# Twelve tile slots in place of six in the expert stage of a gated cross-attention and mixture-of-experts block

## The chip, the cores and the metric

One core of one Trainium2 chip. The metric is the time of the program on the device in microseconds (us), the median of several runs; lower is better.

## The reference

Input `x` has 64 batches of 128 tokens with 128 features. Two residual steps follow each other: cross-attention to a context, then a feed-forward block in which each token goes through one shared expert and one routed expert.

```python
x = x + jnp.tanh(g_xattn[0]) * _L0_xattn_ref(ctx_1024, _layernorm(x, axis=-1), ctx_1024, ...)
x = x + jnp.tanh(g_ffn[0]) * _L0_ffn_ref(_layernorm(x, axis=-1), ...)
...
h = (x - mu) / jnp.sqrt(var + LN_EPS) * ln_gamma + ln_beta
shared_out = jax.nn.silu(jnp.einsum('btd,fd->btf', h, sw1)) @ sw2.T
probs = jax.nn.softmax(h @ router_w.T, axis=-1)
top_prob = jnp.max(probs, axis=-1)
top_idx = jnp.argmax(probs, axis=-1)
h1 = jax.nn.silu(jnp.einsum('btd,efd->ebtf', h, ew1))
eo = jnp.einsum('ebtf,edf->ebtd', h1, ew2)
gate = jax.nn.one_hot(top_idx, N_EXPERTS, dtype=h.dtype) * top_prob[..., None]
routed_out = jnp.einsum('ebtd,bte->btd', eo, gate)
return shared_out + routed_out
```

There are 8 routed experts with 256 hidden features; all expert weights are rounded to three values (-1, 0, 1) times a scale per row.

## The kernel before, in words

The program has two stages. In the attention stage, about the first 420 us of the trace, every batch passes through attention, and each finished token row (128 features, three numbers that its later steps need, and its token number: `ROW` = 132 values) is stored to a buffer in HBM, `rows`, at a place sorted by its expert (`store_rows`, L431). Each expert has a region of its own there.

In the expert stage the sorted rows are worked through as tiles of 128 rows of one expert. There are `NT` = 72 tiles, taken two at a time: 36 pairs, numbered n = 0 to 35. For each pair the engines do this, in this order:

- SP (L291 to L301) reads the two tiles' places from the table `tile_row` and starts two loads from `rows` into slot k of `tin` (L297), 66 KB each. Slot k = n mod `SLOTS`.
- DVE normalises both tiles into `xh` (`normalise_tile`, L754), once the loads have landed.
- PE transposes them (`transpose_tile`, L1284); ACT copies the result to `hT` with the layer norm's gain and offset (`copy_tileT`, L970); DVE splits it in three bf16 parts (`split`, L764).
- PE multiplies with the first-layer weights, shared and routed (`first_layer`, L1292); ACT applies silu (`silus`, L977); PE multiplies with the second layer (`second_layer`, L1311).
- DVE adds both results to the tile in `tin` and writes slot k of `res` (`combine`, L778).
- POOL does a tiny addition into `carrier` (L464), which is held until `res` is there, and then issues two indirect writes of the rows of `res` to `out`, one for each tile, by the token numbers in `tin` (L474). Their landing counts up the semaphore `out_done[k]`.

Each engine has its own program and goes through it strictly in order. All of them write the pairs out in groups of `SLOTS`, with `NG` = 36 / `SLOTS` groups. PE, ACT and DVE have the first and the last group written out and those between as the body of a hardware loop (`Fori`); SP has the first group written out and the others as a loop, POOL has one loop for all groups. A slot number is thus fixed in the code. At the start of a group PE and ACT read the expert numbers of all its tiles from the table `tile_e` into registers with one instruction (L1280 and L997); PE reads the four of the group before again.

On DVE the order within step k is: normalise pair k + 2, split pair k + 1, combine pair k - 1. On PE it is: transpose pair k + 1, first layer of pair k, second layer of pair k - 1. Between the engines the intermediate tiles (`xh`, `hT`, `hpart`, the PSUM banks, `h1s` and `h1r`) have two buffers each, whatever `SLOTS` is; only `tin`, `res` and the semaphores `tile_in` and `out_done` are there once for each slot.

A slot can be loaded again when its results have been written out. This is the wait that SP has in every group but the first:

```python
            def group(g, first=False):
                for k in range(SLOTS):
                    if not first:
                        sp.wait_ge(out_done[k], 32 * g)
                    for a in range(2):
                        row = sp.value_load(tile_row[0:1, bass.ds((g * SLOTS + k) * 2 + a, 1)], ...)
                        sp.dma_start(tin[:, k, a, :], A["rows"][bass.ds(row, P), :]).then_inc(tile_in[k], 16)
```

and this is where DVE waits for the load, at the head of its step:

```python
                dve.wait_ge(tile_in[k], 32 * (g + 1))
                ge(dve, tileT_psum, n - 1)
```

Of the kernel before, what the change touches and what calls it, by code (L numbers as in the profile page):

```python
# [41 lines left out]
PARTS = 3  # L42
MR = P - SK
PAYS = 4
SLOTS = 6
NG = NT // 2 // SLOTS
LAST_SUMS, LAST_PROJ, LAST_RANKS, LAST_LOGITS = 4, 5, 0, 1
SP_PADS = 4
# [10 lines left out]
def build(nc, A):  # L59
    ctx = ExitStack()  # L60
    with ctx:
        def sb(name, shape, dt=FP32):
            return ctx.enter_context(nc.sbuf_tensor(name, shape, dt))

        def sem(name):
            return ctx.enter_context(nc.semaphore(name))
# [114 lines left out]
        h1r = shared[:, 4 * F:8 * F].rearrange("p (s a f c) -> p s a f c", s=2, a=2, f=FB)  # L181
        res = sb("res", [P, SLOTS, 2, D])
        W2T = sb("W2T", [P, NE, FB, P])
        neg = sb("neg", [P, F])
        W1T = sb("W1T", [P, NE, FB, P], BF16)
        tin = sb("tin", [P, SLOTS, 2, ROW])
        rest = sb("rest", [P, 2 * P])
# [36 lines left out]
        pads_out, carried = sem("pads_out"), sem("carried")  # L224
        tile_in = [sem(f"tile_in{k}") for k in range(SLOTS)]
        xh_ready, tileT_psum, tileT_copied, h_part, split_done = (sem(x) for x in ("xh_ready", "tileT_psum", "tileT_copied", "h_part", "split_done"))
        zs_psum, zr_psum, silu_done, y_psum, y_sum, res_ready = (sem(x) for x in ("zs_psum", "zr_psum", "silu_done", "y_psum", "y_sum", "res_ready"))
        out_done = [sem(f"out_done{k}") for k in range(SLOTS)]

# [5 lines left out]
        def _(sp):  # L235
# [55 lines left out]
# [5 lines that stand above are left out]
                        row = sp.value_load(tile_row[0:1, bass.ds((g * SLOTS + k) * 2 + a, 1)], min_val=0, max_val=E * REGION)  # L296
                        sp.dma_start(tin[:, k, a, :], A["rows"][bass.ds(row, P), :]).then_inc(tile_in[k], 16)  # L297
# [1078 lines left out]
```

## Time and profile before

| what | us |
|---|---|
| runs | 582.95, 587.7, 588.3 |
| median of the runs | 587.7 |
| span of the profiled execution | 583.8 |
| attention stage and tables in that span | 0 to about 425 |
| first load of a tile in the expert stage | 425.5 |
| first result handed to POOL | 440.7 |
| last result handed to POOL | 574.4 |

The profile follows one execution of the program. Engines are named PE (matmul), PEld (its weight loads, which overlap PE), DVE, ACT, POOL and SP; a "q" behind a name is the engine's own instruction queue. Times in the trace are counted from the start of the span. The profiled execution's own time is its span, 583.8 us, between the lowest and the median of the three runs and 3.9 us below the median.

### The profile page before, as it was taken

What the parts mean: (1) busy time and instruction counts of PE and PEld (TensorE: products, weight loads), DVE (VectorE), ACT (ScalarE), POOL (GpSimd) and SP (SyncE); (2) the same over time, 40 slices, a digit from 0 to 9 for tenths busy, and PEclk for the clock granted to TensorE, in tenths of its full rate; (3) what the DMA queues carried; (4) which work ended last, traced back from release to release, by engine and by line L of the source; (5) the groups of instructions that cost most, each with busy time, mean ns of one, the idle gap of its engine ahead of it and who ended that gap; (6) DMA issues with size and microseconds to landing.
All of it is one profiled execution on the core that took longest, in us unless ns stands there. A gap on an engine that the chain in (4) does not pass through costs nothing.

```text
span 583.8 us, 22049 instructions
## 1 busy us (share of the span) xinstructions
PE 533.3 (91%) x8243; PEld 438.6 (75%) x8244; DVE 434.6 (74%) x1245; ACT 309.2 (53%) x686; POOL 374.4 (64%) x842
## 2 busy tenths in 40 slices
PE   3869999999999999999999999998889899989991
PEld 1347777878778788888888888886558888888881
DVE  3269666788888889888777777777857777777771
ACT  1415555555555556666565565443136666666660
POOL 7653465476777777877867867767604656565564
PEclk9868999999999999999999999999789999999997
DMA  6900431110211202202202102000221222222210
GB/s 169 244 9 5 135 101 39 57 56 23 67 36 45 72 12 70 72 12 71 62 21 71 55 28 64 13 17 29 85 47 52 67 58 70 69 67 64 71 56 10
DMA packets 53578, 34.61 MB, mean 59 GB/s; under 512 B 6034, under 2 KB 50910, under 8 KB 53488
## 3 DMA queue, kind: packets, MB, share of 16 engines
q1 hardware_dynamic: 47104, 24.38, 15.7%
q0 software_dynamic: 4352, 8.53, 4.4%
q8 instruction: 61, 1.00, 0.7%
q10 hardware_dynamic: 2032, 0.46, 0.4%
q14 instruction: 29, 0.24, 0.1%
HBM read 24.22 MB, written 9.65 MB: 58 GB/s over the span
## 4 chain that ended last, share of the span: by engine, by line
PE 53%; issue 18%; POOL 12%; DVE 10%; DMA 2%; ACT 1%; POOLq 1%; SPq 1%; ACTq 0%; DVEq 0%
PE PS L1108 12%; POOL out L474 9%; PE PS L1078 8%; PE PS L1061 8%; PE PS L1091 7%; PE PS L1048 5%; PE PS L1135 4%; DVE nm L554 2%; DVE rinv L562 2%; POOL rows L434 2%; DVE st L501 2%; PE PS L1069 1%; PE PS L1042 1%; POOL carrier L464 1%; DMA mask_i<-in_mask 1%
## 5 line engine op out<-in xcount | busy, mean ns | idle before, releaser
L894 ACT ACTIVATE shared<-PS 104x768 f32<-104x768 f32 x128 | 103.6, 809 | 62.4 <-PE PS L1091 62.2
L554 DVE TENSOR_REDUCE nm<-PS 128x8 f32<-128x616 f32 x128 | 102.2, 799 | 37.8 <-PE PS L1061 32.0
L1078 PE MATMUL PS<-xT,kbd 32*104 32x128 f32 x1536 | 117.9, 285 | 0.0
L1061 PE MATMUL PS<-kbd,xT 32*128 32x308 f32 x512 | 103.8, 482 | 0.0
L474 POOL DMA_INDIRECT out<-res,tin x72 | 75.0, 1042 | 30.3 <-issue 30.3
L1078 PEld LDWEIGHTS PS<-xT,kbd 32*104 32x104 f32 x1536 | 90.8, 167 | 0.1
L562 DVE RECIPROCAL rinv<-PS 128x128 f32<-128x128 f32 x64 | 61.3, 957 | 25.8 <-PE PS L1108 24.9
L434 POOL DMA_INDIRECT rows<-X,pos_i x64 | 66.0, 1031 | 17.7 <-issue 7.5
L1091 PEld LDWEIGHTS PS<-moving,pairsel 128*104 128x104 bf16 x768 | 56.3, 128 | 15.3 <-issue 12.5
L1091 PE MATMUL PS<-moving,pairsel 128*104 128x128 bf16 x768 | 66.9, 223 | 0.0
L405 POOL CAST nm<-nm 128x16 bf16<-128x16 f32 x64 | 13.3, 208 | 77.4 <-DVE nm L554 77.3
L1048 PE MATMUL PS<-maskneg,identb 128*128 128x308 bf16 x256 | 56.2, 302 | 6.7 <-DVE nm L554 6.5
L1061 PEld LDWEIGHTS PS<-kbd,xT 32*128 32x128 f32 x512 | 39.3, 188 | 22.2 <-issue 17.5
L1108 PE MATMUL PS<-shared,own 104*32 104x128 f32 x1536 | 55.4, 277 | 0.3 <-ACT shared L894 0.3
L1108 PE MATMUL PS<-shared,vm 104*32 104x128 f32 x1536 | 53.6, 273 | 0.0
L985 ACT ACTIVATE shared<-PS,wabs 128x256 f32<-128x256 f32 x72 | 34.0, 474 | 27.2 <-PE PS L1299 19.4
L351 POOL TENSOR_TENSOR kbd<-kp,rowsel 128x308 f32<-128x308 f32 x64 | 44.8, 702 | 2.1 <-ACT kp L883 2.1
L1318 PE MATMUL PS<-W2T,shared 128*128 128x128 f32 x288 | 45.9, 282 | 0.0
L1108 PEld LDWEIGHTS PS<-shared,own 104*32 104x32 f32 x1536 | 38.2, 110 | 9.2 <-ACT shared L894 0.4
L1322 PE MATMUL PS<-W2T,shared 128*128 x288 | 43.9, 275 | 0.0
L1108 PEld LDWEIGHTS PS<-shared,vm 104*32 104x32 f32 x1536 | 43.2, 110 | 0.0
L760 DVE TENSOR_SCALAR xh<-tin 128x128 f32<-128x128 f32 x72 | 22.7, 368 | 26.0 <-DMA tin<-rows 25.9
(202 smaller groups left out, 1093.1 us busy)
## 6 DMA issues: line engine op xcount, KB each, us to landing
ctxq<-in_ctx SPq DMA_DIRECT2D x32, 154.0 KB
tin<-rows SPq DMA_DIRECT2D x72, 66.0 KB, 1.8
X<-in_x SPq DMA_DIRECT2D x8, 512.0 KB, 7.1
ctxp<-in_ctx SPq DMA_DIRECT2D x16, 154.0 KB
ctxq<-in_ctx SPq DMA_DIRECT2D x16, 104.0 KB
ctxq<-in_ctx SPq DMA_DIRECT2D x16, 102.0 KB
out<-res,tin POOLq DMA_INDIRECT x72, 2.3
w2n<-in_ew SPq DMA_DIRECT2D x1, 1024.0 KB, 6.0
```

What stands on the lines that cost most here:

```text
L351: nc.gpsimd.tensor_tensor(kbd[:, q % 2, j, :, 0:SK], kp[:, j].unsqueeze(1).broadcast_to([P, GH, SK]), rowsel[:].unsqueeze(2).broadcast_to( ...
L434: nc.gpsimd.indirect_dma_start(out=A["rows"][:, :], out_offset=row_of(pos_i[:, b:b + 1]), in_=X[:, b, :], in_offset=None).then_inc(sorted_ ...
L474: nc.gpsimd.indirect_dma_start(out=A["out"].rearrange("b q d -> (b q) d"), out_offset=row_of(tin[:, k, a, ROW - 1:ROW]), in_=res[:, k, a, ...
L554: nc.vector.tensor_reduce(nm[:, b % 2, 2 * u * GH:2 * (u + 1) * GH].rearrange("p (g i) -> p g i", g=2), PS[:, 0:2, 0:GK].rearrange("p g (i ...
L562: nc.vector.reciprocal(rinv[:], PS[:, bank, P:2 * P]).then_inc(rinv_done, 1)
L894: nc.scalar.activation(PT[:, b % 2, 2 * u:2 * u + 2, :], PS[0:CR, 2 + 2 * u:4 + 2 * u, 0:CH * P], ACT.Exp, scale=float(1.0 / np.sqrt(HD))) ...
L1048: nc.tensor.matmul(PS[:, v, 0:GK], identb[:], maskneg[:].rearrange("p i k -> p (i k)"), start=True, stop=False)
L1061: ins = nc.tensor.matmul(PS[:, v, 0:GK].rearrange("p (i k) -> p i k", k=SK), xT[r, q % 2, j * P:(j + 1) * P], kbd[r, q % 2, j, :, 0:SK], s ...
L1078: nc.tensor.matmul(PS[0:CR, 2 + g, c * P:(c + 1) * P], kbd[r, q % 2, j].rearrange("p i k -> p (i k)")[:, c * CR:(c + 1) * CR], xT[r, q % 2 ...
L1091: ins = nc.tensor.matmul(PS[0:CR, 2 + g, c * P:(c + 1) * P], pairsel[:, g].rearrange("p i k -> p (i k)")[:, c * CR:(c + 1) * CR], moving[: ...
L1108: ins = nc.tensor.matmul(PS[g * GR:(g + 1) * GR, bank, col:col + P], w[:, c, :] if col else w[:, c, g, :], PT[:, b % 2, g, c * P:(c + 1) * ...
L1318: nc.tensor.matmul(PS[:, 4 + s, 2 * a * P:(2 * a + 1) * P], h1s[:, s, f, a * P:(a + 1) * P], W2T[:, E, f, :], start=f == 0, stop=f == FB - 1)
```

## The change

One constant goes from 6 to 12. With it `tin` and `res` have twelve slots in place of six (and `tile_in` and `out_done` twelve semaphores each), and `NG` goes from six groups of six pairs to three groups of twelve.

```diff
-SLOTS = 6
+SLOTS = 12
 NG = NT // 2 // SLOTS
```

The work on each pair is the same, and so is its order on each engine. What moves are the places where a group ends.

On SP the first group, whose loads wait for nothing, gets twelve more loads before the loop begins. The piece of the difference shows where its written-out part ended before; the four rows with a + come twelve times.

```order
 L297 ISA
 L297 DMA tin<-rows 128x132
+L296 TENSOR_LOAD tile_row
+L296 ISA x2
+L297 ISA
+L297 DMA tin<-rows 128x132
```

So loads 13 to 24 stand without a wait; in the loop behind them the wait on `out_done` is for a write of twelve pairs before, not six.

On PE the loop between the first and the last group was run four times, with counts and waits kept in registers. Before, its first rows were these (the expert numbers, then the transposes of a pair and its first layer):

```order
L1348 UNCONDITIONAL_BRANCH
L1348 ISA
L1280 TENSOR_LOAD tile_e
L1286 ISA
L56 REGISTER_ALU [waits xh_ready]
L1289 MATMUL PS<-ident,xh 128x128 [waits tileT_copied]
L1289 MATMUL PS<-ident,xh 128x128
L56 REGISTER_ALU [waits split_done]
L1299 MATMUL PS<-hpart,W1T 128x256 [waits silu_done]
```

Now the loop is run once, and the same place reads so:

```order
L1348 UNCONDITIONAL_BRANCH
L1280 TENSOR_LOAD tile_e
L1289 MATMUL PS<-ident,xh 128x128 [waits tileT_copied,xh_ready]
L1289 MATMUL PS<-ident,xh 128x128
L1299 MATMUL PS<-hpart,W1T 128x256 [waits silu_done,split_done]
```

The waits are the same and are on constants now; `TENSOR_LOAD` stands three times in a run of the program in place of six, and reads 24 numbers in the first group and 28 in the others, in place of 12 and 16.

## Rows read from the trace of the kernel before

**Rows 1.** Stretches of the span: busy time of each engine, granted clock.

```profile
core 0: us, PE busy (x) PEld busy (x) DVE busy (x) ACT busy (x) POOL busy (x), PEclk, DMA share, GB/s
440.00:568.00 128.00, 116.81 (x1199) 108.22 (x1197) 98.42 (x297) 83.91 (x232) 75.44 (x99) 1.00 0.23 64
440.00:450.00 10.00, 9.87 (x106) 9.46 (x103) 7.23 (x24) 7.37 (x21) 6.59 (x9) 1.00 0.14 41
```

**Rows 2.** Waits in 440 to 584 us: who, for whom, total, times, longest (us).

```profile
POOL carrier L464 <- DVE res L786: 41.8, 33, 18.0
...
DVE xh L760 <- DMA tin<-rows: 22.3, 27, 1.7
...
PE PS L1299 <- DVE hpart L772: 11.0, 20, 1.2
...
PEld PS L1299 <- issue: 2.1, 3, 0.9
```

**Rows 3.** Timeline of POOL: start, length (us), instruction, [idle before <-releaser].

```profile
442.95 0.99 POOL L474 DMA_INDIRECT out<-res,tin  x1 [0.31 <-issue]
444.06 0.22 POOL L464 TENSOR_TENSOR carrier<-rank 128x1 f32<-128x1 f32 x1
...
447.44 0.19 POOL L464 TENSOR_TENSOR carrier<-rank 128x1 f32<-128x1 f32 x1
...
452.22 0.19 POOL L464 TENSOR_TENSOR carrier<-rank 128x1 f32<-128x1 f32 x1 [1.80 <-DVE res L786]
452.94 1.14 POOL L474 DMA_INDIRECT out<-res,tin  x1 [0.53 <-issue]
454.38 1.12 POOL L474 DMA_INDIRECT out<-res,tin  x1 [0.30 <-issue]
...
476.02 0.19 POOL L464 TENSOR_TENSOR carrier<-rank 128x1 f32<-128x1 f32 x1 [1.34 <-DVE res L786]
...
568.20 0.19 POOL L464 TENSOR_TENSOR carrier<-rank 128x1 f32<-128x1 f32 x1 [0.48 <-DVE res L786]
```

**Rows 4.** Timeline of PE: transposes of two pairs that follow, and a late first layer.

```profile
442.70 0.38 PE L1289 MATMUL PS<-ident,xh 128*128 128x128 f32 x2
...
446.08 0.38 PE L1289 MATMUL PS<-ident,xh 128*128 128x128 f32 x2
...
462.93 0.50 PE L1299 MATMUL PS<-hpart,W1T 128*128 128x256 bf16 x3 [1.21 <-DVE hpart L772]
```

**Rows 5.** Timeline of DVE: one step early in the stage, and a later one.

```profile
440.50 0.59 DVE L760 TENSOR_SCALAR xh<-tin 128x128 f32<-128x128 f32 x2
...
442.90 0.42 DVE L783 TENSOR_TENSOR res<-tin,PS 128x256 f32<-128x256 f32 x1 [0.36 <-PE PS L1322]
...
443.88 0.34 DVE L760 TENSOR_SCALAR xh<-tin 128x128 f32<-128x128 f32 x1
...
460.62 0.61 DVE L760 TENSOR_SCALAR xh<-tin 128x128 f32<-128x128 f32 x2 [1.40 <-DMA tin<-rows]
```

**Rows 6.** Timeline of SP: the first twelve loads, and the two of pair 9.

```profile
425.49 12.86 SPq L297 DMA_DIRECT2D tin<-rows  x12
...
457.60 1.52 SPq L297 DMA_DIRECT2D tin<-rows  x2
```

**Rows 7.** Single lines of the kernel: duration ns min/median/max, first and last start (us).

```profile
L474 POOL DMA_INDIRECT out<-res,tin x72: 966/992/1237, 441.4 to 576.0; - x72
...
L760 DVE TENSOR_SCALAR xh<-tin x72: 334/346/603, 428.5 to 561.6; 128x128 f32<-128x128 f32 x72
...
L770 DVE CAST hpart<-hT x36: 274/286/466, 431.3 to 564.5; 128x256 bf16<-128x256 f32 x36
L770 DVE CAST hpart<-rest x36: 293/295/552, 432.1 to 565.3; 128x256 bf16<-128x256 f32 x36
...
L1280 PEldq TENSOR_LOAD <-tile_e x6: 1036/1112/1125, 429.3 to 546.3; - x6
```

## The prediction

> **What bounds the kernel now.** I read the table of stretches first. In the expert stage, 440 to 568 us, TensorE is busy for 116.81 of 128 us at a granted clock of 1.00, its upper level of 2.4 GHz; in the first ten of these it is busy for 9.87 of 10 [rows 1]. So for its first pairs the stage is bound by PE, and then something takes about a tenth away.
>
> The table of waits names it. DVE waits 22.3 us in 27 waits for tile loads, PE's first layer then waits 11.0 us for DVE's split, and POOL waits for DVE's results [rows 2]. DVE does its steps in order, and the wait for the load of pair k + 2 stands at the head of the step, ahead of the split that PE needs next. A late load thus stops PE, though its own tile is wanted only a step later: at 460.62 DVE begins to normalise pair 9 after 1.40 us of waiting for its load [rows 5], and at 462.93 PE begins the first layer of the pair before, 1.21 us late [rows 4].
>
> The timelines show the pace. POOL's small addition, `carrier`, marks when a pair's result is there. Counted from pair 0 at 440.7, it stands at 444.06 for pair 1, 447.44 for pair 2 and 452.22 for pair 3 [rows 3]. The 3.38 us between the first two are PE's own pace: its transposes of two pairs that follow start at 442.70 and 446.08, which is 3.38 apart, with no wait in the list [rows 4]. From pair 2 at 447.44 to pair 33 at 568.20 [rows 3] there are 31 steps in 120.76 us, 3.90 each. So 0.52 us a step is lost after pair 2.
>
> Why the loads are late: a slot's load has to wait for the write of the pair six before. Followed for one slot: the result of pair 3 reaches POOL at 452.22; POOL's two writes are issued by 454.38 + 1.12 = 455.50 [rows 3]; they land, and SP starts the loads of pair 9 at 457.60 [rows 6], 2.10 later; DVE normalises pair 9 at 460.62 [rows 5], 3.02 later; its result reaches POOL at 476.02 [rows 3], 15.40 later. That is 23.80 us for a turn of one slot, and six pairs pass in a turn: 3.97 us a pair. The ring of slots is longer than six of PE's steps (6 x 3.38 = 20.28), and this sets the pace.
>
> **The change part by part.** Twelve slots: the same turn of 23.80 us is now shared by twelve pairs, 1.98 us a pair, well under PE's 3.38. The loads also come early enough at the start. The first twelve are issued in 12.86 us with nothing to wait for [rows 6], hence about 1.14 us each; 24 of them go on at that pace, and the two of pair 6 start by 425.49 + 13 x 1.14 = 440.3. From the first load's start to the normalising of pair 9 it was 3.02 us, with both loads in it, so pair 6 is in the slot before 442.5. DVE would take it one step after 443.88 [rows 5], at 447.26. From then on SP stays about 5 pairs ahead. So DVE's 22.3 us of load waits go.
>
> What is late next is PE. Its step has no gap at 3.38 us; DVE's step in the same place, 440.50 to 443.88, holds 0.36 us of waiting for PE [rows 5], so DVE needs 3.02; ACT is busy 83.91 us of 128 with 33 to 34 pairs in it [rows 1], some 2.5 us each. POOL needs, from 444.06 on, until its second write is issued; with the pair before as model the second write ended at 442.95 + 0.99 = 443.94 and the next addition began 0.12 later [rows 3], so POOL was nearly full there too, and still kept PE's pace. At that pace pair 33 reaches POOL at 447.44 + 31 x 3.38 = 552.22 in place of 568.20: 15.98 us less. Behind it the last two pairs and the end of the program are as before.
>
> The edges of the groups: a jump into the loop and the table read L1280 now stand at two places behind the first pair, where there were five. A read takes 1036 to 1125 ns [rows 7], the low end with 12 numbers and the high end with 16, about 20 ns a number, so with 28 about 1.36 us (an estimate from these). PE's sequencer runs ahead of the array, so that much of it is covered by the second layer of the pair before; the trace shows 2.1 us of waits on PE's own issue, in 3 places [rows 2], over five edges: 0.42 each. Bounds for an edge: 0 if it is covered, 1.36 if none of it is. I take 0.42, the row that shows it, so 0.84 for two; both ends give 0 to 2.7.
>
> The registers that carried counts in the loop are constants now; the additions on them were done by sequencers that ran ahead, and I put them at nothing. The attention stage is the same code. The longer code is executed once in place of a loop of four turns; the first group is such code already and runs at 3.38, so its fetching costs nothing unless the trace of after shows issue waits.
>
> Sum: 15.98 - 0.84 = 15.1 us. On the profiled execution 583.8 - 15.1 = 568.7. The median of the runs is 3.9 above that execution, and the part outside the expert stage that makes runs differ is not touched, so 587.7 - 15.1 = 572.6.
>
> **A rule that speaks against it.** A write's issue on POOL takes 966 ns at least and 1237 at most, and DVE's normalising 334 to 603 [rows 7]: one of them stretches at times, by about 0.26 us, when both run. In the Trainium skill, page "SBUF — State Buffer", section "Who interferes with whom", GpSimd and certain two-port operations of DVE, casts and scalar operations among them, take a shared port pair in turn, and the one that comes second is blocked for the whole instruction. The trace agrees as far as these spreads go. With DVE's waiting gone, its operations would meet POOL's more often, and by the page POOL, with the least room, could become the bound; the price of that is worked out next, from rows.
>
> **The rivals.** *POOL becomes the bound (12 in 100).* If every write's issue met DVE, POOL's step would be the addition and the gap behind it (452.94 - 452.22 = 0.72), two issues at the most each (1.24), 0.30 between them, and 0.12 before the next [rows 3, 7]: 3.62 us, 0.24 over PE's. Over 31 steps the gain falls by 31 x 0.24 = 7.4 us: 580.0. For it: POOL was nearly full already between pairs 1 and 2. Against it: one of the two issues there was 0.99, and the pace was PE's. With twelve slots POOL may fall behind by some pairs without stopping SP, so a few long issues only add to the end.
>
> *DVE becomes the bound, and it is slower (3 in 100).* If the shared resource held up DVE instead, each of its two normalisings (0.60 for 0.35) and its two casts (0.47 for 0.29, 0.55 for 0.30) at the longest seen [rows 7], its step would grow by 2 x 0.26 + 0.18 + 0.26 = 0.96 from 3.02 to 3.98. Over 31 steps that is 123.4 us against 120.76, 2.6 slower, and with edges at their top 5.3: 593.0. It decides from 0.88 us of growth a step, 3.90 less 3.02. Against it: in the first pairs these operations stood at their medians while POOL was writing.
>
> *The loads stay late (4 in 100).* If the wait were for the loads' own speed and not for the slot, more slots would buy nothing: 587.7. For it: DVE waited for loads at the very start, when no slot was waited for. Against it: SP issues a pair in 2.28 us unhindered [rows 6], below 3.38, and pairs 4 and 5 were taken without a wait.
>
> **How the numbers follow.** The forecast, 572.6, has 81 in 100, POOL as bound 12, late loads 4, DVE as bound 3. The forecast's own range is from 15.98 saved without cost at the edges and a run at the low end (582.95 - 16.0 = 567.0) to edges at the top (574.4) on a run at the high end, 575. POOL as bound reaches 580.0, so the range is 566.5 to 580. A measurement of this kernel tells about 1%, 5.9 us, from no change. The forecast and POOL as bound lie beyond that on the fast side, 93; late loads are within it, 4, and of DVE's case the third in which it grows by little more than 0.88 us, so 5; slower by over that 2.
>
> **What would show it.** Right: DVE's waits for loads are gone behind pair 3; SP waits on `out_done`, and nobody waits for SP; the `carrier` rows are 3.38 to 3.45 apart up to pair 33; PE is busy for 9.8 of every 10 us. POOL as bound: `carrier` rows without idle ahead and PE on pace, the last rows of POOL bunched and late. DVE as bound: PE's first layer waits for the split with no load wait behind it. Edges dearer than said: issue waits of PE over 0.5 us at pairs 12 and 24. Wrong altogether: load waits at DVE that go on behind pair 6.

## The result, and the profile after

The changed kernel takes 570.45 us (median; 569.13 to 570.69), the kernel before 588.0 us (582.95 to 593.16, with one more run than was known ahead). The ratio is 0.9715 with a 95% interval of 0.9679 to 0.9751: 2.9% faster, 15 to 19 us. 572.6 us was forecast. The profiled execution of after has a span of 568.4 us and a time of its own of 570.28.

The expert stage of after, with the columns of [rows 1], shows where the time came from:

```profile
440.00:552.00 112.00, 111.42 (x1185) 108.52 (x1183) 94.23 (x294) 83.53 (x231) 78.42 (x99) 1.00 0.27 74
```

TensorE is busy for 99.5% of the expert stage now; before it was 91%. What is done is the same, it is only done without gaps.

The waits of after from 440 us to the end; who, for whom, total, times, longest [rows 2]:

```profile
POOL carrier L464 <- DVE res L786: 22.5, 29, 16.9
ACT hT L974 <- PE PS L1289: 19.2, 33, 1.1
DVE res L783 <- PE PS L1322: 16.1, 35, 2.1
...
PE PS L1289 <- issue: 0.6, 2, 0.4
```

DVE's wait for loads, 22.3 us before, is not in the list any more, nor is PE's wait for the split. The other engines wait for PE now. All that PE waits for is its own issue, in two places.

POOL's `carrier` rows [rows 3]: pair 2, pairs 10 and 11, pairs 22 and 23, pairs 25 and 26, pair 33.

```profile
447.36 0.22 POOL L464 TENSOR_TENSOR carrier<-rank 128x1 f32<-128x1 f32 x1
...
474.42 0.22 POOL L464 TENSOR_TENSOR carrier<-rank 128x1 f32<-128x1 f32 x1 [0.15 <-DVE res L786]
478.35 0.22 POOL L464 TENSOR_TENSOR carrier<-rank 128x1 f32<-128x1 f32 x1 [0.70 <-DVE res L786]
...
515.57 0.22 POOL L464 TENSOR_TENSOR carrier<-rank 128x1 f32<-128x1 f32 x1 [0.15 <-DVE res L786]
519.37 0.22 POOL L464 TENSOR_TENSOR carrier<-rank 128x1 f32<-128x1 f32 x1 [0.57 <-DVE res L786]
...
526.56 0.25 POOL L464 TENSOR_TENSOR carrier<-rank 128x1 f32<-128x1 f32 x1
...
529.52 0.22 POOL L464 TENSOR_TENSOR carrier<-rank 128x1 f32<-128x1 f32 x1 [0.16 <-DVE res L786]
...
553.20 0.19 POOL L464 TENSOR_TENSOR carrier<-rank 128x1 f32<-128x1 f32 x1 [0.34 <-DVE res L786]
```

From pair 2 to pair 33 it is 105.84 us, against 120.76. Nearly every step is 3.38. The two in which PE itself loses time are the edges of the groups, 3.93 and 3.80: 0.55 and 0.42 more. One other is longer, the 3.81 up to pair 25: there POOL was late by itself, and the next step, 2.96, makes it good.

SP, with its row up to 470 us [rows 6] and its wait on the semaphores of the writes:

```profile
426.45 43.19 SPq L297 DMA_DIRECT2D tin<-rows  x38
...
SPq L296 <- DMA out<-res,tin: 15.9, 11, 3.0
```

It issues these 38 loads, those of pairs 0 to 18, at 1.14 us each, the pace of the first twelve before. Its waits for writes in the loop (L296) come to 15.9 us, most of them later, and nobody waits for it.

Durations of after [rows 7]:

```profile
L474 POOL DMA_INDIRECT out<-res,tin x72: 971/990/1237, 441.3 to 561.0; - x72
L760 DVE TENSOR_SCALAR xh<-tin x72: 334/340/381, 429.4 to 546.5; 128x128 f32<-128x128 f32 x72
L770 DVE CAST hpart<-rest x36: 293/293/295, 432.9 to 550.4; 128x256 bf16<-128x256 f32 x36
L1280 PEldq TENSOR_LOAD <-tile_e x3: 1807/1881/2092, 430.2 to 512.6; - x3
```

### The profile page after: what moved, and what is told of

It reads as the page before. It is cut to its first block, busy times and chain, and to the rows that moved or that the text cites. A ratio compares the mean times of both kernels' runs of the same rounds, so it can differ in the third digit from the quotient of the medians.

```text
span 568.4 us, 21827 instructions
## 1 busy us (share of the span) xinstructions
PE 526.3 (93%) x8243; PEld 438.8 (77%) x8243; DVE 430.9 (76%) x1245; ACT 309.2 (54%) x685; POOL 378.3 (67%) x842
## 4 chain that ended last, share of the span: by engine, by line
PE 54%; issue 16%; POOL 12%; DVE 11%; DMA 2%; ACT 2%; SPq 1%; POOLq 1%; ACTq 0%; DVEq 0%
PE PS L1108 12%; POOL out L474 8%; PE PS L1061 8%; PE PS L1078 8%; PE PS L1091 8%; PE PS L1048 5%; PE PS L1135 4%; DVE nm L554 3%; DVE st L501 2%; DVE rinv L562 2%; POOL rows L434 2%; PE PS L1069 1%; PE PS L1042 1%; POOL carrier L464 1%; DMA ctxp<-in_ctx 1%
## 5 line engine op out<-in xcount | busy, mean ns | idle before, releaser
L474 POOL DMA_INDIRECT out<-res,tin x72 | 78.0, 1083 | 29.5 <-issue 29.5
L1091 PEld LDWEIGHTS PS<-moving,pairsel 128*104 128x104 bf16 x768 | 56.5, 128 | 15.4 <-issue 12.7
L988 ACT ACTIVATE shared<-PS,wabs 128x128 f32<-128x128 f32 x144 | 40.8, 372 | 0.0
```

Source lines behind the costliest of these rows:

```text
L474: nc.gpsimd.indirect_dma_start(out=A["out"].rearrange("b q d -> (b q) d"), out_offset=row_of(tin[:, k, a, ROW - 1:ROW]), in_=res[:, k, a, ...
L1091: ins = nc.tensor.matmul(PS[0:CR, 2 + g, c * P:(c + 1) * P], pairsel[:, g].rearrange("p i k -> p (i k)")[:, c * CR:(c + 1) * CR], moving[: ...
```

## The experiments

The theory: a ring of slots (load, compute, write out, load again) set the pace of the stage, and with twelve slots PE does. The first four runs keep the changed kernel, its twelve slots and its three long groups, and put back the wait alone, at a distance d of pairs. DVE normalises pair n before it combines pair n - 3, so a distance of 3 would wait for itself, and 4 is the least. The edit, here for d = 6:

```diff
-                    if not first:
-                        sp.wait_ge(out_done[k], 32 * g)
+                    if k >= 6:
+                        sp.wait_ge(out_done[k - 6], 32 * (g + 1))
+                    elif not first:
+                        sp.wait_ge(out_done[k + SLOTS - 6], 32 * g)
```

**The wait on pair n - 6 (wait6).**

> Twelve slots and three groups of twelve pairs as in the changed kernel; only the wait of SP is put back: the load of pair n waits for the write of pair n - 6 again. Theory (the turn from a pair's result over its write to the load that waited for it sets the pace): the carrier rows are 3.8 to 3.95 us apart from pair 6 on, DVE waits some 20 us for loads again, about 586 us, within 1% of the kernel before. Rival (the gain is from the longer groups, the constants in place of registers and the fewer loop edges): the rows stay 3.38 apart and the time stays at 570 to 571 us. Mixed: in between, and the share tells how much is due to each.

Measured: 589.98 us, ratio to the kernel before 1.0061 (1.0029 to 1.0094). Its `carrier` rows of pairs 2, 3 and 33, and its wait for loads:

```profile
446.92 0.19 POOL L466 TENSOR_TENSOR carrier<-rank 128x1 f32<-128x1 f32 x1
451.70 0.19 POOL L466 TENSOR_TENSOR carrier<-rank 128x1 f32<-128x1 f32 x1 [1.79 <-DVE res L788]
...
573.73 0.19 POOL L466 TENSOR_TENSOR carrier<-rank 128x1 f32<-128x1 f32 x1 [0.43 <-DVE res L788]
...
DVE xh L762 <- DMA tin<-rows: 22.9, 22, 2.7
```

With one wait put back the whole gain is gone: 126.81 us for the 31 steps, and 22.9 us of load waits. Longer groups, constants and fewer edges give nothing by themselves. The steps are 4.09 us, even 0.19 longer than before, which the expectation did not have; the last experiment is on that too.

**The wait on pair n - 7 (wait7).**

> As wait6, with the wait on the write of pair n - 7. Theory: the turn allows 11.5 to 11.7 us for four steps, 2.9 us a step, under PE's 3.38, so one more slot than six gives the whole gain: 570 to 572 us, rows 3.38 apart, no load waits at DVE beyond the start (with the turn taken as a constant 23.8 us it would be 3.40 a pair, which is the same within noise). Rival (each slot brings its share, a sixth of the gain): about 585 us.

Measured: 570.99 us, ratio 0.976 (0.9733 to 0.9786), which is after within its noise. Pairs 2 and 33, and the wait for loads:

```profile
447.81 0.22 POOL L466 TENSOR_TENSOR carrier<-rank 128x1 f32<-128x1 f32 x1
...
554.09 0.19 POOL L466 TENSOR_TENSOR carrier<-rank 128x1 f32<-128x1 f32 x1 [0.34 <-DVE res L788]
...
DVE xh L762 <- DMA tin<-rows: 0.6, 2, 0.4
```

The 31 steps take 106.28 us, against 105.84 with a distance of twelve. One slot more than six gives all of it; the rival by which each slot brings its share is out. Seven has little room to spare: 0.6 us of load waits are left.

**The waits on pairs n - 5 and n - 4 (wait5, wait4).**

> As wait6, with the wait on the write of pair n - 5. Two forms of the theory differ here. Turn with steps in it (write and load 8.4 us and some 3.1 us of DVE have to fit in the steps that lie between, of which n - 5 leaves two): 5.7 to 5.9 us a pair, about 570.5 + 30 x 2.4 = 640 to 645 us. Constant turn of 23.8 us shared by five: 4.76 a pair, about 611 us. If the loads' distance did not matter: 570.5 us.

> As wait6, with the wait on the write of pair n - 4. Turn with steps in it: only one step lies between, so 11.4 to 11.7 us a pair, about 570.5 + 31 x 8.15 = 820 to 830 us. Constant turn of 23.8 us shared by four: 5.95 a pair, about 650 us. If the loads' distance did not matter: 570.5 us.

Measured, one run each: 648.07 us with five and 823.62 us with four. The loads wait 83.0 and 263.6 us in total. The form with steps in it holds (3 us over its range with five, within it with four); a constant turn, with 611 and 650, does not. One turn of the ring, with four:

```profile
462.68 0.19 POOL L466 TENSOR_TENSOR carrier<-rank 128x1 f32<-128x1 f32 x1 [8.10 <-DVE res L788]
...
464.70 0.97 POOL L476 DMA_INDIRECT out<-res,tin  x1 [0.30 <-issue]
...
467.68 1.44 SPq L299 DMA_DIRECT2D tin<-rows  x2
...
470.68 0.60 DVE L762 TENSOR_SCALAR xh<-tin 128x128 f32<-128x128 f32 x2 [8.09 <-DMA tin<-rows]
...
473.80 0.19 POOL L466 TENSOR_TENSOR carrier<-rank 128x1 f32<-128x1 f32 x1 [8.13 <-DVE res L788]
```

Here everything else stands still, so the fixed part can be read off: 2.99 us for the two writes' issue, 2.01 until they have landed and SP starts the next load, 3.00 until DVE has both tiles, 3.12 for DVE's step. That is 11.12 us for one step. With five there are two steps between, with six three, with seven four: 5.56, 3.71, 2.78. Measured from pair 2 to pair 33: 11.1 (462.68 to 806.63), 5.77 (452.21 to 631.08), 4.09 (3.90 in the kernel before), and with seven PE's 3.43 with its edges. The step to pair 33 waits for no load any more; without it the first two are 11.27 and 5.84. So the form is a floor, and the runs with five and six lie 0.2 to 0.4 us a step above it.

**PE's read of the expert numbers in two parts (reads_in_two).**

```diff
-                experts = load_experts(0, 2 * SLOTS) if first else load_experts(2 * SLOTS * g - 4, 2 * SLOTS + 4)
+                half = SLOTS // 2
+                experts = load_experts(0, SLOTS) if first else load_experts(2 * SLOTS * g - 4, SLOTS + 4)
...
                 for k in range(SLOTS):
+                    if k == half:
+                        experts = [*experts, *load_experts(2 * SLOTS * g + SLOTS, SLOTS)]
```

> The changed kernel, with PE's read of a group's expert numbers cut in two: the first six pairs' numbers at the edge (12, or 16 with the four of the group before), the other 12 six pairs later. Theory (at the two edges the read of 28 numbers, 1.9 to 2.1 us, is longer than the work that PE's queue still holds, and costs 0.4 to 0.55 us): reads of 1.04 to 1.12 us, all covered, the carrier rows 3.38 apart over the edges too, 1.0 us less in the span, 569.5 us. Rival (the edge costs because of the jump or of code that is not there yet): the 0.4 to 0.55 us stay at the edges, 570.4 us. A difference of 1 us is near what five rounds tell; the rows at the edges decide.

Measured: 569.92 us, ratio 0.969 (0.9638 to 0.9742). By time it can't be told from after. The rows of pairs 2, 11, 12 and 33, over the first edge and to the end, and the reads:

```profile
448.96 0.22 POOL L464 TENSOR_TENSOR carrier<-rank 128x1 f32<-128x1 f32 x1
...
479.42 0.22 POOL L464 TENSOR_TENSOR carrier<-rank 128x1 f32<-128x1 f32 x1 [0.15 <-DVE res L786]
482.80 0.22 POOL L464 TENSOR_TENSOR carrier<-rank 128x1 f32<-128x1 f32 x1 [0.16 <-DVE res L786]
...
553.85 0.19 POOL L464 TENSOR_TENSOR carrier<-rank 128x1 f32<-128x1 f32 x1 [0.34 <-DVE res L786]
...
L1280 PEldq TENSOR_LOAD <-tile_e x6: 872/990/1197, 430.4 to 533.8; - x6
```

The 31 steps take 104.89 us, 3.383 each, and neither edge costs time any more. So the edges cost what the long read takes beyond PE's queued work, and not the jump. The expected 0.95 us is there in the stage; the stage began 1.6 us later in this execution, and so the span does not show it. This is the version that I would keep, though its gain over after is below what the runs tell.

**PE's step made shorter (pe_less).**

```diff
-                    for h in range(3):
+                    for h in (0, 1):
...
-                                               start=h == 0, stop=h == 2)
+                                               start=h == 0, stop=h == 1)
```

(the same in the loop over the routed experts)

> The changed kernel without the third bf16 part of the normalised tile in both first layers (six of 18 first-layer matmuls on PE left out, so the output is a little less exact); DVE still makes that part. It takes 2 x 0.109 + 4 x 0.056 = 0.44 us from PE's step of 3.38. Theory (PE alone bounds the step now, POOL is next at 3.2): rows 3.2 to 3.25 apart, POOL without idle time, 4.5 to 6 us less, 565 us. If POOL had more room than I think, DVE is next at 3.02: 559 us. Rival (PE is not what bounds, the pace is set by something that is in step with it): 570.5 us.

Measured: 558.02 us, ratio 0.9484 (0.9417 to 0.9551): 12 us below after. PE did bound the step. That the next bound is POOL at 3.2 was wrong. A step of POOL and one of DVE, with its second cast:

```profile
482.30 0.50 POOL L464 TENSOR_TENSOR carrier<-rank 128x1 f32<-128x1 f32 x1
482.96 1.13 POOL L474 DMA_INDIRECT out<-res,tin  x1 [0.16 <-issue]
484.39 0.97 POOL L474 DMA_INDIRECT out<-res,tin  x1 [0.30 <-issue]
485.38 0.36 POOL L464 TENSOR_TENSOR carrier<-rank 128x1 f32<-128x1 f32 x1
...
481.96 0.59 DVE L760 TENSOR_SCALAR xh<-tin 128x128 f32<-128x128 f32 x2
...
483.25 0.29 DVE L770 CAST hpart<-rest 128x256 bf16<-128x256 f32 x1
...
483.93 0.42 DVE L783 TENSOR_TENSOR res<-tin,PS 128x256 f32<-128x256 f32 x1
...
484.91 0.51 DVE L760 TENSOR_SCALAR xh<-tin 128x128 f32<-128x128 f32 x1
```

DVE goes through its 2.95 us without a gap (its wait for PE, [0.36] in [rows 5], is gone), POOL needs 3.08 here, and a step over the stage is 94.62 / 31 = 3.05 (pairs 2 and 33 at 448.58 and 543.20), edges included. PE with 2.94 (its transposes at 480.78 and 483.72), DVE and POOL are then within 0.15 us of each other, and which of them sets the pace is not told apart.

**More work on POOL (pool_more).**

```diff
-                    carry(g * SLOTS + k)
+                    for i in range(2):
+                        carry(2 * SLOTS * g + 2 * k + i)
```

> The changed kernel with POOL's small addition done twice for each pair, 0.22 us and its own wait more. Theory (POOL has 0.15 to 0.2 us of room in a step): POOL's step becomes 3.5 to 3.7 us, it falls behind PE by that from pair to pair without stopping it, and ends 4 to 10 us later: 575 to 580 us; the carrier rows stand without idle time ahead of them. Rival (POOL has room for it, or what it loses is made up): 570.5 us.

Measured: 571.43 us, ratio 0.973 (0.9663 to 0.9798): not to be told from after, so the rival holds. A step of POOL, and DVE's second cast in it:

```profile
482.84 0.60 POOL L464 TENSOR_TENSOR carrier<-rank 128x1 f32<-128x1 f32 x2
483.83 0.99 POOL L475 DMA_INDIRECT out<-res,tin  x1 [0.40 <-issue]
483.88 0.29 DVE L771 CAST hpart<-rest 128x256 bf16<-128x256 f32 x1
...
486.23 0.59 POOL L464 TENSOR_TENSOR carrier<-rank 128x1 f32<-128x1 f32 x2
```

The addition is there, but the first write takes 0.99 us where after has 1.24, since it now starts at another point of DVE's step. Part of what looked like POOL's work in a full step was stretch, and it gives way.

**The loops written out, with six slots (unrolled6).**

```diff
-            with pe.Fori(0, NG - 2) as gi:
+            for gi in range(NG - 2):
```

(the same for DVE and ACT, in the kernel before)

> The kernel before, six slots, with the loops of PE, ACT and DVE over the four middle groups written out; SP and POOL keep theirs. Theory: the ring of six slots still sets the pace, no gain. Its second part, formed after the run with the wait on pair n - 6 put back came out slower than the kernel before (4.09 a pair in place of 3.90): between 473.5 and 554 us the kernel before, in its loop, loads no instructions at all, and code that is written out loads a block every few us; a transfer of tiles or results that is under way then lands 1 to 2 us later, and a ring that is the bound passes that on. By that: blocks of instructions from 440 to 570 us, loads that land 2 us and more behind the usual, 4.0 to 4.1 us a pair, 588 to 592 us. Rival: the slower steps of that run came from SP's longer waits on registers: 3.90 a pair and 585 to 588 us here. Rival of the gain itself (constants and fewer edges give it): under 580 us.

Measured: 589.72 us, ratio to the kernel before 1.004 (1.0001 to 1.0078). No gain, as expected; 122.9 us for the 31 steps (449.29 to 572.21), 3.96 each, between the two forecasts of 3.90 and 4.0. Blocks of instructions are loaded all through its stage, where the kernel before loads none from 473.5 to 554 us, as expected (below).

What makes these two runs slower by 0.4 and 0.6% can be read off the traces. From the end of the issue of a pair's second write to its landing it is 1.28 us as a rule, from the start of its second load to its landing 1.84. In the ten traces, 368 such landings had no block of instructions (code that is fetched by DMA while the program runs) under way beside them, and none of these took longer than 1.78 us (writes) or 2.02 (loads). Of 351 with one beside them, 122 did, up to 3.41 and 3.63. Two windows of wait6 show it. In the first, 511.9 to 514.6 us, the second write of pair 17 has one block beside it and lands 4.2 us after its issue began; in the other, 505.9 to 508.5, the second write of pair 16 has none and lands after 2.2.

```profile
q8 instruction: 1, 0.02, 2.1%
...
out<-res,tin POOLq DMA_INDIRECT x1, 4.2
```

```profile
out<-res,tin POOLq DMA_INDIRECT x1, 2.2
```

A late landing of pair n's write makes the load of pair n + 6 late and, through DVE's step, the result of pair n + 3. In wait6 the writes of pairs 2, 11, 14 and 17 took 2.77, 2.76, 2.46 and 3.27 us; they follow in steps of three, so their excess adds up, 6.1 us. The 31 steps are 6.05 us longer than before. In unrolled6 the loads of pairs 19 and 22, with 3.42 and 2.32, make 2.1 of the 2.2 us by which its 31 steps are longer. This is a rough reckoning from one trace of each run (the kernel before has one such write itself, pair 5's with 2.23); that the blocks hold the transfers up is the likely reading of it, not shown by itself. SP's different waits in wait6 can be a small part at most: from a landing to the start of the load that waited for it, it is 0.82 us in the median in both kernels. In after the same late landings occur, up to 3.41 and 3.60 us, and DVE waits for none.

## Why the prediction was right

**The ring as the bound.** Right, and shown by wait6 against wait7: one wait makes or undoes the whole gain. The sum took 31 steps from 3.90 to 3.38, 15.98 us; 105.84 less the edges' 0.97 leaves 104.87, 15.89.

**The price of the edges.** 0.42 each was taken, 0.55 and 0.42 measured. The ground for it was partly wrong, and that the price came out so near is partly luck: the 2.1 us were three waits of PE's weight loads, spread over five edges, for reads of 16 numbers. The estimate for a read of 28 numbers was 1.36 us, by the slope between 12 and 16; it took 1.88 and more [after's L1280 row]. That the cost stayed small was because PE's queue covered about 1.5 us of it (2.09 less 0.55 at the first edge, 1.88 less 0.42 at the second).

**The form of the turn.** "The same turn of 23.80 us is now shared by twelve pairs" gave the right answer with the wrong formula. A turn holds steps of the kernel itself, which stretch when the ring is late. What is fixed is 11.1 us, and it has to fit in d - 3 steps. With twelve both forms lie far under 3.38, so the forecast did not depend on it; with five and four the first form is wrong by 37 and 174 us.

**POOL "nearly full".** This is the step that failed, without harm to the number. POOL's 0.12 ahead of the addition and 0.50 before the first write were read as its own time; in pe_less, where the result is there before POOL is, the gap before the write is 0.16 and the step 2.95 to 3.08. The row of after shows it too: POOL's step from pair 25 to pair 26 is 2.96. The rival at 3.62 a step, with 12 in 100, had too high a price.

**DVE as bound, and the shared port.** In after, normalising takes 381 ns at most and casts 295, where they reached 603 and 552 before. The collisions that were to become more frequent became regular: in a steady step it is POOL's first write that is stretched, from 0.99 to 1.23 or 1.24 us, and DVE is not. Such a step of after, the write and DVE's second cast:

```profile
458.22 1.23 POOL L474 DMA_INDIRECT out<-res,tin  x1 [0.50 <-issue]
...
458.62 0.29 DVE L770 CAST hpart<-rest 128x256 bf16<-128x256 f32 x1
```

The stretch depends on when the cast begins behind the start of the write: after 0.40 us here, and the write takes 1.23; after 0.29 in pe_less, 1.13; after 0.05 in pool_more, where the write starts 0.27 us later behind `carrier`, 0.99 and no stretch. In both stretched cases the write ends 0.54 to 0.55 us behind the end of the cast, as if some part of it had to wait until the cast was over. The rule of the Trainium skill that was weighed (page "SBUF — State Buffer", "Who interferes with whom"), by which the one that comes second waits until the first one's instruction is over, agrees with these rows only if the write needs the shared ports some time after its start. That fits pool_more, where the cast is over 0.34 us behind the write's start and holds nothing up.

**The absolute time.** The two profiled spans, 583.8 and 568.4, differ by 15.4 us, against 15.1 forecast, and 14.92 of it lies between pairs 2 and 33. The time itself, 572.6, was 2.2 us too high, since 3.9 us were put between an execution's span and the median. For after's profiled execution its own time lies 1.9 above its span, and the median 0.2 above that time. An execution's time is thus not its span, as was said ahead of the prediction: in every run that has both on record it lies 1.7 to 2.0 above. The rest of the 3.9 was the spread of the kernel before, which was taken to lie outside the expert stage. That does not fit the runs: kernels that the ring bounds (before, wait6, unrolled6) spread by 5 to 8 us, and after, wait7, pool_more and reads_in_two, with the same attention stage, by 1.2 to 2.8, in fewer runs. Late landings are a candidate for it, not shown.

## What to carry to other kernels

Where a buffer is loaded, used and written out from the same slot, count the slots by a step without other limits: fixed part (issue of the write, landing, issue and landing of the load, the engine's step) over the number of steps that lie between. It is a floor. Here 11.1 us over 3 steps is more than PE's 3.38 and over 4 less, so a seventh slot is worth 3% and the eighth to twelfth nothing (seen as distances of the wait, in a kernel with twelve). A wait at the head of an in-order engine's step stops work that does not depend on it, so it is the late load's neighbours that lose the time.

## What the runs showed of the hardware that I had not expected

A read of registers by one instruction took 1.04 us for 12 numbers, 1.12 for 16, 1.81 for 24 and 1.88 to 2.09 for 28: it jumps somewhere above 16. In two parts it took 0.87 to 1.20 each.

The code of the loop was not loaded again while it ran. From 473.5 to 554 us the queues of the kernel before are these, with no instruction queue among them (queue, kind: packets, MB, share of 16 engines); behind them stand the instruction queues of after, and then those of unrolled6:

```profile
q1 hardware_dynamic: 6048, 2.84, 15.0%
q0 software_dynamic: 1344, 2.55, 9.4%
```

```profile
q8 instruction: 7, 0.11, 0.6%
q14 instruction: 5, 0.04, 0.2%
```

```profile
q8 instruction: 7, 0.11, 0.5%
q14 instruction: 3, 0.02, 0.1%
```

Writes and loads landed up to 2.1 us later than usual when such a block was under way, and never by more than 0.5 us without one (the last experiment).

With four slots PE stood still for so long in each step that its granted clock fell: a mean of 0.69 from 460 to 800 us, between the lower level of 1.2 GHz and the upper of 2.4, where it is 1.00 in after; the pace was that of the ring all the same.

```profile
460.00:800.00 340.00, 183.92 (x1084) 155.12 (x1084) 88.37 (x276) 77.00 (x211) 64.66 (x90) 0.69 0.09 24
```
